# Rounding of the gated layer's weights pipelined over pieces and spread over the rotary heads; squares of the last attention folded to 64 rows

## The reference, cut to what matters

```python
# first attention (32 heads of 128, a bias per head, mask)
score = einsum(q, k) + position_bias;  out = softmax(where(m, score, -inf)) @ v @ w_out.T
# third attention (32 query heads, 8 key/value heads, rotary), then the gated layer:
q = q * cos + rotate_half(q) * sin;  k = k * cos + rotate_half(k) * sin
def nf4_quant_dequant(w):                       # w1, w2 (1376 x 512), w3 (512 x 1376)
    flat = w.reshape(-1, 64)
    absmax = max(abs(flat), axis=1)
    normalized = flat / where(absmax == 0, 1, absmax)
    idx = searchsorted(bounds, normalized)      # 15 bounds, 16 codes
    return (NF4_CODE[idx] * absmax).reshape(w.shape)
out = (silu(x @ dq1.T) * (x @ dq2.T)) @ dq3.T
# last attention (32 query heads, 8 key/value heads over context and latents)
q = rms_norm(q, q_norm_w);  k = rms_norm(k, k_norm_w)     # over the 128 channels of a head
out = softmax(q @ k.T / sqrt(128)) @ v @ Wo
```

## Time and profile before

| | |
|---|---|
| median of three runs | 3140.89 us (3140.7 to 3143.68) |
| the profiled execution | 3129.63 us, its span 3127.9 us |
| PE busy | 2876.8 us (92%) |
| weight loads (PEld) busy | 2478.2 us (79%) |
| DVE busy | 1994.3 us (64%) |
| ACT busy | 1376.1 us (44%) |
| POOL busy | 1322.3 us (42%) |
| bias, rotary, latent attention | 0 to 905, 1200 to 1893, 2106 to 3010 us of the span |

### The profile page before, as it was taken

How to read it: one execution, slowest core, us unless ns; L and a number is a source line. 1 busy time by engine, 2 the same in 40 slices (tenths; PEclk the granted TensorE clock), 3 DMA queues, 4 the chain that set the end, 5 groups by cost and what they waited for, 6 DMA issues and landing times. The chain is left out here.

```text
span 3127.9 us, 44736 instructions
## 1 busy us (share of the span) xinstructions
PE 2876.8 (92%) x16404; PEld 2478.2 (79%) x16404; DVE 1994.3 (64%) x3493; ACT 1376.1 (44%) x3393; POOL 1322.3 (42%) x1178
## 2 busy tenths in 40 slices
PE   7999999999876886969999998998999999999967
PEld 6888888888765764758888886877999999999946
DVE  5777777778765787878988875345444444444453
ACT  3656556565521553234444432214434444443520
POOL 6455535544422653455555540004434434343420
PEclk9999999999987997989999999999999999999978
DMA  4112112112121002011111103101000101000000
GB/s 134 46 58 64 59 44 64 60 50 65 39 82 46 11 4 65 27 40 43 40 41 41 39 21 115 41 11 41 28 18 28 28 18 29 27 28 18 17 28 27
DMA packets 77832, 131.85 MB, mean 42 GB/s; under 512 B 10025, under 2 KB 23601, under 8 KB 77233
## 3 DMA queue, kind: packets, MB, share of 16 engines
q1 hardware_dynamic: 68112, 112.10, 11.7%
q10 hardware_dynamic: 9504, 16.91, 1.7%
HBM read 114.23 MB, written 14.75 MB: 41 GB/s over the span
## 5 line engine op out<-in xcount | busy, mean ns | idle before, releaser
L89 PE MATMUL a_pa<-a_wo,a_ot 128*128 128x512 f32 x2304 | 538.1, 391 | 9.6 <-issue 7.5
L89 PEld LDWEIGHTS a_pa<-a_wo,a_ot 128*128 128x128 f32 x2304 | 429.7, 188 | 104.6 <-issue 13.0
L362 DVE SCALAR_TENSOR_TENSOR a_nf_acc<-a_nf_t,a_nf_acc 128x512 f32<-128x512 bf16 (+1 forms) x462 | 403.1, 873 | 42.4 <-ACT a_nf_t L316 11.4
L316 ACT ACTIVATE a_nf_t<-a_nf_w,a_nf_shifts 128x512 bf16<-128x512 f32 (+1 forms) x495 | 321.7, 709 | 202.8 <-DVE a_nf_w L346 173.1
L89 PE MATMUL a_pa<-h_t,a_wqk 128*128 128x512 f32 x1536 | 373.7, 396 | 1.7 <-DVE h_t L773 1.7
L89 PEld LDWEIGHTS a_pa<-h_t,a_wqk 128*128 128x128 f32 x1536 | 282.3, 189 | 56.5 <-DVE h_t L773 1.9
L89 PE MATMUL a_pa<-a_wv,ctx_t 128*128 128x512 f32 x960 | 234.0, 400 | 30.6 <-POOL a_wv L532 15.7
L89 PE MATMUL a_pa<-ctx_t,a_wqk 128*128 128x512 f32 x960 | 227.5, 393 | 21.5 <-POOL a_wqk L1651 21.2
L89 PEld LDWEIGHTS a_pa<-a_wv,ctx_t 128*128 128x128 f32 x960 | 181.4, 192 | 68.6 <-POOL a_wv L1651 15.7
L89 PEld LDWEIGHTS a_pa<-ctx_t,a_wqk 128*128 128x128 f32 x960 | 181.7, 190 | 61.0 <-POOL a_wqk L1651 23.2
L1009 POOL TENSOR_TENSOR a_prob<-a_prob,a_inv 128x512 f32<-128x512 f32 x128 | 130.4, 1040 | 181.1 <-DVE a_inv L1375 181.1
(11 more groups left out here) (356 smaller groups left out, 6008.5 us busy)
## 6 DMA issues: line engine op xcount, KB each, us to landing
a_raw<-in_a_w SPq DMA_DIRECT2D x288, 256.0 KB, 2.6
a_nf_w<-in_nf ACTq DMA_DIRECT2D x32, 256.0 KB, 2.7
nf_rounded<-a_nf_acc ACTq DMA_DIRECT2D x32, 256.0 KB, 2.0
f_rows<-nf_rounded SPq DMA_DIRECT2D x22, 256.0 KB, 2.9
ctx_kept<-ctx_t SPq DMA_DIRECT2D x1, 4096.0 KB, 17.2
ctx_t<-ctx_kept SPq DMA_DIRECT2D x1, 4096.0 KB
f_cols<-nf_rounded SPq DMA_DIRECT2D x11, 256.0 KB, 3.7
a_ctx_raw<-in_ctxt SPq DMA_DIRECT2D x4, 512.0 KB, 6.5
```

Of the source, the lines that this page charges most:

```text
L89: ins = nc.tensor.matmul(out, lhs(a), rhs(b), start=first and i == 0, stop=last and i == 2)
L316: self.nc.scalar.activation(self.t[:, m % NF4_RING, cols], self.w[:, p % 2, cols], ACT.Identity, bias=self.shifts[:, u - 2:u - 1], scale=s ...
L362: ins = nc.vector.scalar_tensor_tensor(acc, t, c, acc, inner, outer)
```

## The change

**Rounding.** A generator `units` gives the units in another order: behind the step of unit 9 of a piece come units 0 and 1 of the next piece, and then units 10 to 17. `top` gets two buffers. Unit 0 waits for `v_ready` of the piece before (for `inv`) and for `done` of the one before that (for `top`).

**Where units are issued.** In the bias attention DVE does two units ahead of the heads. In the rotary attention the 24 units ahead of key head 4 become 2 on DVE and 2 (which hold no instruction) on ACT, and `side` gives 3, 1, 2 in heads 0 to 9 and 2, 1, 2 in the rest.

**Squares of the latent attention.** ACT writes four squares of 64 x 512 a head in place of two of 128 x 512: the tokens of half 0 in rows 0 to 63 and those of half 1 in rows 64 to 127, the two halves of the channels side by side. DVE adds the two (`fold_squares`), and PE sums with four matmuls of two moving columns (`sides`). POOL sets `sides` with three memsets in a row, in place of one of `ones`.

**Order on PE in the latent attention.** An output waits for its own half of the weighed values only. In heads 3, 7, ..., 27 the first half of the queries of h + 2 comes ahead of the scores of h + 1.

```diff
+    def units(self, start, count):
+        for n in range(start, start + count):
+            if n < 2:
+                yield 0, n
+                continue
+            p, u = (n - 2) // NF4_UNITS, (n - 2) % NF4_UNITS
+            if u < 8:
+                p, u = p, u + 2
+            elif u < 10:
+                p, u = p + 1, u - 8
+            if p < len(self.sizes):
+                yield p, u
...
-        for unit in range(self.dve_at, min(self.dve_at + count, len(self.sizes) * NF4_UNITS)):
-            p, u = unit // NF4_UNITS, unit % NF4_UNITS
+        for p, u in self.units(self.dve_at, count):
...
-            top, inv = self.top[:, 0:blocks], self.inv[:, 0:blocks]
+            top, inv = self.top[:, p % 2, 0:blocks], self.inv[:, 0:blocks]
...
                 if p > 0:
-                    dve.wait_ge(self.done, p)
+                    dve.wait_ge(self.v_ready, p)
+                if p > 1:
+                    dve.wait_ge(self.done, p - 1)
...  # bias attention, DVE
             inverse(0, 1)
+            rounding.on_vector(dve, 2)
             for h in range(H):
...  # latent attention, POOL
-            nc.gpsimd.memset(ones[:, :], 1.0).then_inc(const_set, 1)
+            nc.gpsimd.memset(sides[:, :], 0.0).then_inc(const_set, 1)
+            for side in range(2):
+                pool.wait_ge(const_set, side + 2)
+                nc.gpsimd.memset(sides[64 * side:64 * side + 64, side:side + 1], 1.0).then_inc(const_set, 1)
...  # latent attention, PE
-                pe.wait_ge(squared, 2 * head + 2)
-                for b in range(NB):
-                    ins = nc.tensor.matmul(out[:, b:b + 1], q2[:, b * P:(b + 1) * P], ones[:, :], start=True, stop=True)
+                pe.wait_ge(folded, head + 1)
+                for i in range(4):
+                    ins = nc.tensor.matmul(out[:, 2 * i:2 * i + 2], q2[:, 0, i * P:(i + 1) * P], sides[:, :],
+                                           start=True, stop=True)
...
             def output(n, b):
+                pe.wait_ge(o_taken, 4 * n + 3 + b // 4)
...
+                if h % 4 == 3 and h + 2 < H:
+                    queries(h + 2, 0)
                 if h + 1 < H:
                     scores(h + 1, 0)
                     scores(h + 1, 1)
-                if h + 2 < H:
+                if h % 4 != 3 and h + 2 < H:
                     queries(h + 2, 0)
...
                     pe.wait_ge(split_done, split_count["o", h])
-                    pe.wait_ge(o_taken, 2 * h + 2)
...  # latent attention, ACT
-                nc.scalar.activation(q2[:, cols], bank(key), ACT.Square).then_inc(squared, 1)
+                for rows in range(2):
+                    nc.scalar.activation(q2[64 * half:64 * half + 64, rows, :], bank(key)[64 * rows:64 * rows + 64, :],
+                                         ACT.Square).then_inc(squared, 1)
...  # latent attention, DVE; called ahead of rest_of_queries(h + 2, 1)
+            def fold_squares(head):
+                dve.wait_ge(squared, 4 * head + 4)
+                nc.vector.tensor_tensor(q2[:, 0, :], q2[:, 0, :], q2[:, 1, :], ALU.add).then_inc(folded, 1)
...  # rotary attention
     def side(step):
-        return (2, 1, 2) if step < 14 else (2, 0, 2)
+        return (3, 1, 2) if step < 10 else (2, 1, 2)
...
-            rounding.on_scalar(act, 3 * NB)
+            rounding.on_scalar(act, 2)
...
-            rounding.on_vector(dve, 3 * NB)
+            rounding.on_vector(dve, 2)
```

More of the change, by code:

```diff
@@ L269, in __init__ @@
         self.acc = at("nf_acc", [P, 2, cols])
-        self.top = at("nf_top", [P, blocks])
+        self.top = at("nf_top", [P, 2, blocks])
         self.inv = at("nf_inv", [P, blocks])
@@ L295, in store @@
         act.dma_start(self.rounded[:, self.columns(p)], self.acc[:, p % 2, 0:self.width(p)]).then_inc(self.stored[p % 2], 16)
+    def units(self, start, count):
[10 more added lines that the diff above has]
+                yield p, u
     def on_scalar(self, act, count):
-        for unit in range(self.act_at, min(self.act_at + count, len(self.sizes) * NF4_UNITS)):
-            p, u = unit // NF4_UNITS, unit % NF4_UNITS
+        for p, u in self.units(self.act_at, count):
             if u < 2:
@@ L923, in latent_attention_stage @@
     raw = at(108 * KB, "raw", [P, 4, D])
-    q2 = at(116 * KB, "q2", [P, NT])
+    q2 = at(116 * KB, "q2", [P, 2, BANK])
     kn = at(120 * KB, "kn", [P, 2, 4, P])
@@ L936, in latent_attention_stage @@
     kss, kms, krs = (next_at(n, [P, 2, 4]) for n in ("kss", "kms", "krs"))
-    ones, kw, kqw = next_at("ones", [P, 1]), next_at("kw", [P, 1]), next_at("kqw", [P, 2])
+    sides, kw, kqw = next_at("sides", [P, 2]), next_at("kw", [P, 1]), next_at("kqw", [P, 2])
     space = next_at("space", [P, 11 * NB])
@@ L1022, in _ @@
             nc.gpsimd.memset(half[:, :], -0.5).then_inc(const_set, 1)
-            nc.gpsimd.memset(ones[:, :], 1.0).then_inc(const_set, 1)
+            nc.gpsimd.memset(sides[:, :], 0.0).then_inc(const_set, 1)
+            for side in range(2):
+                pool.wait_ge(const_set, side + 2)
+                nc.gpsimd.memset(sides[64 * side:64 * side + 64, side:side + 1], 1.0).then_inc(const_set, 1)
+            pool.wait_ge(const_set, 4)
             split(("k", 0))
             split(("v", 0))
-            pool.wait_ge(const_set, 2)
+            pool.wait_ge(const_set, 4)
             norm.rstd_on_gpsimd(nc, pool)
@@ L1169, in _ @@
             turned_keys(0, 3)
-            pe.wait_ge(const_set, 2)
+            pe.wait_ge(const_set, 4)
             squares_of_queries(0)
@@ L1358, in mean_squares @@
                 dve.wait_ge(a_ready, made_count[key])
-                nc.vector.tensor_scalar(qms[:, :], bank(key)[:, 0:NB], P * 1e-6, None, ALU.add).then_inc(ss_ready, 1)
+                nc.vector.tensor_scalar(qms[:, :].rearrange("p (s i) -> p i s", s=2),
+                                        bank(key)[:, 0:NB].rearrange("p (i s) -> p i s", s=2), P * 1e-6, None, ALU.add
+                                        ).then_inc(ss_ready, 1)
                 dve.wait_ge(ss_ready, head + 1)
@@ L1388, in add_output @@
                 nc.vector.tensor_tensor(x[:, b, :], bank(key), x[:, b, :], ALU.add).then_inc(taken, 1)
-            dve.wait_ge(const_set, 2)
+            dve.wait_ge(const_set, 4)
             norm.stats_on_vector(nc, Steps(dve, own_norm), x)
@@ L1409, in _ @@
             rest_of_queries(0, 0)
+            fold_squares(0)
             rest_of_queries(0, 1)
@@ L1420, in _ @@
             inverse(0, 1)
+            fold_squares(1)
             rest_of_queries(1, 1)
@@ L1447, in _ @@
                 if h + 2 < H:
+                    fold_squares(h + 2)
                     rest_of_queries(h + 2, 1)
```

4 lines of the change are left out of this document (2 added, 2 removed).

## The result

The changed kernel takes 3183.41 us (median of four, 3175.86 to 3185.83) against 3140.80 (3137.28 to 3143.68) for the kernel before on the same chip: ratio 1.0132, interval 1.0112 to 1.0152. It is 1.3% slower; I had forecast 3098.7 and gave "slower" 0.04. The profiled execution has a span of 3181.6 us. Where an execution ran at a lower clock throughout it is left out of the ratio; there was one, of 4155.8 us in experiment 1.

The account below looks back on a forecast made before the run. PE was taken to bound all three attentions. Gains of 13 us (bias), 21.8 less 5.5 (rotary) and 12.9 (latent) sum to 42.2, giving 3087.4, or 3098.7 on the median; eight-in-ten range 3074 to 3119.

Parts of the forecast that it names:

- the two units ahead of the heads: Bias attention: DVE's two early units cost nothing, as DVE is idle 7.49 us there; otherwise head 1's shifts 3.8 us late.
- the ring: Bias attention: ACT can be only four steps ahead of DVE; five of PE's waits, 5.6 us, come from this and stay.
- Rival 3: Rotary heads 0 to 9: DVE's lateness feeds itself, PE's waits reach 3.5 us; 57 us lost, 3156; chance 0.04.
- the new order: Bias attention: reordered rounding units end ACT's stops at the start of a piece; gain 13 us, bounds 5 and 26.
- Head 29: Bias attention: PE's wait for the copy of k falls from 8.66 to 2 us; 6 us gained there.
- rival 1: All stages: the cover holds everywhere, no new waits and the ring waits gone; 69 us gained, 3072; chance 0.17.
- a wait of 2 us has no such trail: Rotary key head 6: with the wait shrunk, no slow matmuls follow it, so 2.8 us more come back.
- The fuller heads: Rotary heads: the 22 units moved into them cost 5.5 us, bounds 0 and 10.
- The wait for `keep_values`: Latent attention: after the shorter squares PE waits 0.28 us in each of 27 heads, 7.7 us together.
- The first head's fold: Start of the latent attention: the fold and second square add 0.8 us to the first head's chain.
- The order in every fourth head: Latent attention: queries ahead of scores lose a 0.69 us wait but cost 1.3; net loss 4.3 us in seven heads.
- outputs by half: Latent attention: they keep odd heads from a new wait; worth about nothing against before.

Follow-up runs that it names:

- experiment 1: The kernel after, without the two units of rounding that DVE does ahead of the bias attention's heads: 3083.78 us, ratio 0.9823.
- experiment 3: The kernel before, with only DVE's two units ahead of the bias attention's heads added: 3241.28 us, ratio 1.0326.
- experiment 7: kernel 2 with the queries of every fourth latent head again behind the scores: 3076.53 us (0.9811), run again 3081.84 (0.9817) beside kernel 2's 3081.99 (0.9818).
- experiment 8: kernel 2 with the latent outputs of odd heads again behind one wait for both halves of the weighed values: 3087.53 us, ratio 0.9847.
- 4: The kernel after, with DVE's one unit between shifts and inverses moved behind both inverses in each bias attention head: 3109.07 us, ratio 0.9904.
- 6: The kernel after, with five ACT units ahead of the bias attention's heads in place of two, and the old latent order of queries: 3076.91 us, ratio 0.9800.
- 9: kernel 2 with the old latent order of queries and, in every fourth head, the third transposes ahead of the scores: 3078.29 us, ratio 0.9806.
- kernel 2: The kernel after, with four ACT units ahead of the bias attention's heads in place of two: 3079.13 us, ratio 0.9813.

## Why the prediction was wrong, step by step

**Bias attention, the two units ahead of the heads: the step that failed.** "The two units ahead of the heads cost nothing: DVE is idle 7.49 us there." I priced them where they stand. Their price lies in every head behind, since they shift DVE's place in the order of units against ACT's. They cost 100 us in the kernel after (experiment 1) and 103 in the kernel before (experiment 3): 51 us of PE's waits and 28 of slower matmuls after, and the gain that they hid. I had read how far ACT can run ahead of DVE (the ring), never how far it has to be ahead at each place where DVE's stream asks for a step. No rival had it either. Rival 3 came nearest, with DVE late, inverses late and PE's waits reaching 3.5 us at a lower clock, but it stood in the rotary heads, at 57 us, and its cause was DVE's own sum of work, not a wait for ACT. The chance of 0.04 that I gave to "slower" was given for another reason than the one that came true.

What made it readable beforehand: a wait of zero is a row too. DVE's unit at 99.99 follows the shift of 99.92 without idle time, and with ACT's next step only at 103.59 it relied on one of the head before.

**Bias attention, the new order: right in kind, too small.** With the lead given back the stage gains 23.8 us (925.9 less 902.1) where I took 13, within the bounds of 5 to 26 (23.8 lies near the upper one). The five waits that I kept as coming from the ring went as well: PE's waits for k fall from 20.5 to 4.4, those for `x` from 2.0 to none, and PE is busy 5.5 us less for the same work. Head 29 came out short of my reckoning (4.4 left, forecast 2). It was rival 1's value for this stage (23).

**Rotary attention: right, with two terms that cancel.** The timeline of PE after, which answers the earlier trace rows:

```profile
1420.27 7.38 PE L89 MATMUL a_pa<-ctx_t,a_wqk 128*128 128x512 f32 x24 [2.24 <-POOL a_wqk L1684]
1427.49 5.60 PE L89 MATMUL a_pa<-h_t,a_wqk 128*128 128x512 f32 x24
```

The wait is 2.24 us (forecast 2.3): 19.0 gained. The slow matmuls behind it don't vanish: 7.38 in place of 8.55 us, 1.2 gained where I took 2.8. That "a wait of 2 us has no such trail" was read from one wait of 1.73 us, and was wrong here: PE's granted clock from 1422 to 1424 is 0.50, its lower level. The fuller heads cost less: PE's unnamed waits of the heads grow from 4.5 to 7.7 us, mostly ahead of the outputs of heads 3, 5, 7 and 9 (0.73, 1.00, 1.94 and 0.74 us), and the wait for the rotated queries by 0.5, 3.7 together where I took 5.5. 20.2 less 3.7 is 16.5, and the marks give 16.3. DVE did not become the bound: it is busy 170.6 of the 190 us from 1450 to 1640, in the heads with six units.

**Latent attention: right, nearly term by term.** Two heads after, which answer and the earlier trace rows:

```profile
2376.40 0.95 PE L1124 MATMUL a_pa<-a_sides,a_q 128*128 128x2 f32 x8
2377.52 0.65 PE L1109 MATMUL a_pa<-ident,a_kn 128*128 128x128 f32 x4 [0.17 <-ACT a_v L1256]
...
2397.46 0.95 PE L1124 MATMUL a_pa<-a_sides,a_q 128*128 128x2 f32 x8
2398.67 11.17 PE L89 MATMUL a_pa<-a_wo,a_ot 128*128 128x512 f32 x48 [0.27 <-ACT a_v L1256]
```

The 256 records are there. The wait for `keep_values` that no row of before showed is there, in each of the 27 heads, 0.17 to 0.27 us (forecast 0.28). The waits of PE in the stage:

```profile
PE a_pscore L89 <- ACT a_prob L1277: 5.7, 8, 0.7
PE a_pa L89 <- ACT a_v L1256: 3.4, 13, 0.3
...
PE a_pa L1109 <- ACT a_v L1256: 2.4, 14, 0.2
PE a_pa L1124 <- DVE a_q L1382: 2.1, 2, 1.9
```

5.8 us of waits for `keep_values` where I took 7.7. The profile counts them from the end of the squares; counted as I did, from the start of the squares to the next start, it is 1.12 us in an even head and 1.21 in an odd one, where I took 1.14 (2308.38 to 2309.52). The first head's fold costs more than the 0.8 I took: PE waits 1.9 us for it, the matmuls behind run slower, and from the first matmul of the keys and values from `h_t` to the second head's squares it is 38.02 us (2207.34 to 2245.36) in place of 35.30, so 2.7. The order in every fourth head costs 3.3 us by experiment 7, where I took 4.3. That the outputs by half are "worth about nothing against before" holds, since before had no wait there; as a part of this change they are worth 8 to 10 us (experiment 8), which I hadn't said.

**The sum.** -16.3 and -13.8 stand against my -16.3 and -12.9; that the rotary one agrees to a tenth is luck, since two of its terms were off by 1.6 and 1.8 us the opposite way. With the lead kept, the time would have been some 16 to 20 us under the forecast (3079.1, or 0.9813 of 3140.9, against 3098.7), most of it in the bias attention, and the range would have held it. The range reached 3119; for the step that failed it held nothing, and the one cost named for it was shifts 3.8 us late in head 1.

## What to carry to other kernels

Where two engines walk through one sequence of side work in streams written by hand, count for each engine how many units it has issued at every place where it can be asked for one. The difference, not either count, is the margin, and adding work to one side ahead of a loop moves it in every pass of the loop. A side unit placed ahead of work that others wait for must be one whose input is already queued before the loop's own waits; test it by shifting the other engine's count by one.

And a place where the trace of before shows no wait is evidence that some slack is used there. Ask what the slack is before spending it.

## What the runs showed of the hardware

**A long GpSimd operation held up DVE by 4 to 5 us, and whether it did hung on half a microsecond.** 5.1 of the 84 us have nothing to do with the rounding. Behind the bias attention, DVE makes eight scalings of the norm (L130), while POOL splits weights that have just been loaded. After:

```profile
992.12 10.75 DVE L130 TENSOR_SCALAR f_norm_h<-x,f_norm_space 128x512 f32<-128x512 f32 x8 [1.86 <-POOL f_norm_space L127]
...
996.64 4.54 POOL L2194 TENSOR_TENSOR f_base<-f_raw,f_base 128x2048 fp32r<-128x2048 f32 x1
```

Before:

```profile
913.42 5.62 DVE L130 TENSOR_SCALAR f_norm_h<-x,f_norm_space 128x512 f32<-128x512 f32 x8 [1.86 <-POOL f_norm_space L127]
...
918.85 4.58 POOL L2161 TENSOR_TENSOR f_base<-f_raw,f_base 128x2048 fp32r<-128x2048 f32 x1
```

POOL's operation begins 5.43 us behind the first scaling before, when the last scaling is under way, and 4.52 us behind it after, when one or two are still to come; the next one ends only with POOL's 4.54 us, and one scaling has 4.7 us in place of 0.54. In all fourteen profiles the rule is the same: begun 4.05 to 4.98 us behind (after, experiments 1, 4, 6, 9 and both runs of 7) the eight take 9.8 or 10.7 us, begun 5.43 us behind or later (the other seven) they take 5.3 to 5.6. The Trainium skill (SBUF — State Buffer, Who interferes with whom) calls the pair of ports that DVE and GpSimd share an exclusive lock; these rows agree, and they show that a scaling with one SBUF input can be the one that is locked out. PE waits 7.2 us in place of 2.1 for it. When POOL begins is set by a DMA's landing, so an edit in another stage can bring this in or take it away: in the profiles of experiment 7 it came and went with the order of the latent attention, a later stage, and how that reaches the landing stays open.

**The same contention grew with the lateness of the bias attention.** DVE's steps of the rounding took 1021 ns in the mean after against 889 before, and 876 in kernel 2; the 128x4 product in `inverse` 540 ns against 205 in kernel 2. With the inverses late, POOL's normalisation begins in the middle of DVE's second inverse and beside its steps. The first makes 44 of the 61 us that DVE was busier in that stage. In head 1 DVE's second product in `inverse` began 0.04 us behind POOL's normalisation of 110.39 and took 1.02 us, where the first took 0.16. It is a consequence of the lost lead, since it goes with it; how much of PE's waits it made was not separated.

**A wait of 2 to 2.5 us of PE was followed by half the clock in some executions and not in others, so stages differ more than the kernels compared here.** Kernel 2 was profiled twice: its rotary stretch took 959.0 and 963.9 us, its latent one 1144.2 and 1148.1. Of the last 3.9 us, 2.8 come from one place. Between the squares of heads 1 and 2 PE waits 2.52 us for the turned keys in both; behind the wait the granted clock is 1.00 (2.4 GHz) in the first profile and 0.50 (1.2 GHz) from 2148.4 to 2153.0 us in the second, where twelve matmuls of the scores take 2.91 us in place of 1.68. The start of the latent attention has two such states as well: the 96 matmuls of the keys and values from `h_t` take 11.8 us or 13.3 to 13.5, and from `f_ptr` to the first squares the kernels with the fold need 260.6 to 261.5 us in seven profiles and 263.7 to 264.8 in five. What sets the state is open. Passes 1 to 29 of the same code repeat within 0.1 us, so effects of a few us are read between two marks inside the loop, and not from a stage time.
